# A transformer block with 16 top-1 experts: a memory region per expert, routing and row scatters inside the attention pipeline, unsplit expert weights, return by gathers

## The chip, the cores and the metric

The kernel runs on one NeuronCore of a Trainium2 chip. Its engines are TensorE (PE, with its weight loads shown as PEld), VectorE (DVE), ScalarE (ACT), GpSimd (POOL) and the queue of SyncE (SP), which issues most of the plain DMAs; ACT and POOL issue DMAs too. They run side by side and meet at semaphores. The metric is the device time of one execution in microseconds; the kernel before takes 283.23 us (median of 3 runs, 281.55 to 284.89).

## The reference

The input `x` is 4 sequences of 1024 tokens with 128 features, so T = 4096 rows. Two layers follow each other, each behind a LayerNorm and each added to its input:

```
q, k = l2norm(heads(n @ Wq + bq)), l2norm(heads(n @ Wk + bk)); v = heads(n @ Wv + bv)
attn = (q k^T) / 1024 ** sigmoid(m)            # 16 heads of 8, no softmax
x    = x + (attn v) @ Wo + bo
h    = layernorm(x)
logits = h @ router_w.T                         # 16 experts, top 1
score  = sigmoid(logit of the chosen expert)
g, u = split((h * score) @ gate_up[e]);  routed = (u * silu(g)) @ down[e]
shared = (silu(h @ shared_gate.T) * (h @ shared_up.T)) @ shared_down.T     # inner width 512
out  = x + shared + routed
```

Attention is linear (no softmax), so q (k^T v) is computed as 128x128 products.

## The kernel before

**Units.** 4096 tokens are 32 tiles of 128 rows and 8 quads of 4 tiles. A stage works on a quad at a time (512 columns). The shared part takes a quad in KC = 4 steps, so 32 steps in all. The routed part sorts rows by expert into slots of 128 rows, each slot of one expert; NG = 12 groups of 4 slots always suffice (48 slots).

**Order of the program.** The order is written out by hand for each engine and stands still; semaphores alone couple the engines.

1. *Attention*, STEPS = 11 steps `s` over the 8 quads, software pipelined: step `s` projects quad `s` (PE `project`, L932), DVE takes q, k, v out of PSUM (`take_qkv`, L682), sums squares per head (L691), floors them with a max (L695) and inverts the roots (L699); POOL scales q and v (`scale_heads`, L378); PE multiplies k by v and, three steps later, attends (`attend`, L970); DVE adds the result to `xres` (L711) and makes the second LayerNorm's scales (L668). POOL also adds the bias `bo` to `xres` (`add_bo`, L387), makes the low half of `hT` (`hT_lo`, L391) and, in steps 2, 4, 6 and 8, of the expert weights (`split_lo`, L397): every fp32 operand of `split_product` (L976 to L978) is held as a high and a low fp32r half, and a product is three passes. ACT makes the high halves (`split_hi`, L519).
2. *Routing*, once for quads 0 to 5 and once for 6 and 7: DVE picks the largest logit (`choose`, L777 to L786), counts rows ahead of each row (L789 to L793) and places them (L797 to L800). POOL and ACT scale the rows of `h_rows` by their score (L405).
3. *Scatters of the rows*: POOL issues 32 indirect DMAs (L432), a tile each, from `h_rows` to `x_slots` in memory. Tile t waits until tile t-2 has landed, so at most two are under way:

```
for t in range(NT):
    ...
    if t >= 2:
        pool.wait_ge(scat[t % 2], 16 * (t // 2))
    g.indirect_dma_start(out=x_slots, ..., in_=h_rows[:, t, :], ...).then_inc(scat[t % 2], 16)
```

   Beside them PE, ACT and DVE run the shared part for C1 = 5 quads (`silu_shared` L534, `act_shared` L726, `lo_shared` L731, `down_shared` L1014 to L1016, `turn_y` L1065, `add_shared` L848).
4. *Experts*, 12 groups: SP loads a group when all scatters have landed (one DMA of 258 KB), PE transposes it (L1108), gate-up product in split form (L976 to L978), ACT silu (L619), DVE product (L889), PE transposes (L1132), DVE copies (L893), PE down product (L1124), ACT copy into `yg` (L623). Each group's result goes back by 4 indirect DMAs on POOL (L441) to the rows of its tokens in `y_rows`, paced as the first scatters are, behind the same ring of two.
5. *The other 3 shared quads*, and when all 48 result scatters have landed, SP loads `y_rows` in 8 straight DMAs, POOL adds quads 0 to 3 (L447) and DVE quads 4 to 7 (`add_experts`, L843), and `out` is stored.

In the rows below, `x_slots` and `y_rows` are tensors in memory, `bank` is one of four PSUM banks, `quad_banks` the other four, `pos` the row of `x_slots` that a token goes to, `home` the row that a result returns to.

## Time and profile before

| what | value |
|---|---|
| median of 3 runs | 283.23 us |
| profiled execution: span from first to last instruction | 289.3 us |
| mean granted TensorE clock | 0.863 of full |
| busy: PE, DVE, POOL, ACT | 205.9, 166.4, 142.6, 123.6 us |
| POOL, issues of y scatters (L441) | 48, 46.6 us |
| POOL, issues of x scatters (L432) | 32, 32.5 us |

The span stands for the time of the profiled execution; nothing outside it is listed. It is 6.1 us above the median of the runs. PE is the busiest engine over the whole, at 71%, but the share is an average over stages that have different limits, which the windows below take apart. The page's chain of waits gives PE 22%, DVE 19%, "issue" (time that the profile gives no reason for) 19%, an unknown releaser 14%, POOL 12%.

### The profile page before, as it was taken

What the parts mean: (1) busy time and instruction counts of PE and PEld (TensorE: products, weight loads), DVE (VectorE), ACT (ScalarE), POOL (GpSimd) and SP (SyncE); (2) the same over time, 40 slices, a digit from 0 to 9 for tenths busy, and PEclk for the clock granted to TensorE, in tenths of its full rate; (3) what the DMA queues carried; (4) which work ended last, traced back from release to release, by engine and by line L of the source; (5) the groups of instructions that cost most, each with busy time, mean ns of one, the idle gap of its engine ahead of it and who ended that gap; (6) DMA issues with size and microseconds to landing.
All of it is one profiled execution on the core that took longest, in us unless ns stands there. A gap on an engine that the chain in (4) does not pass through costs nothing.

```text
span 289.3 us, 3485 instructions
## 1 busy us (share of the span) xinstructions
PE 205.9 (71%) x1067; PEld 164.8 (57%) x1067; DVE 166.4 (58%) x401; ACT 123.6 (43%) x238; POOL 142.6 (49%) x148
## 2 busy tenths in 40 slices
PE   1777868898897694889996005999866733539983
PEld 0435646667687573567774004999865632427761
DVE  2179999989863869966667001775832100124665
ACT  3325458565664778355555001454521101024560
POOL 8004747556564227356666640045567666752610
PEclk9999999978975976899999555999997567669999
DMA  4997020520000000011111114244311110102935
GB/s 127 293 386 250 6 70 1 160 60 1 1 2 0 0 0 0 11 39 46 37 48 37 46 37 110 73 106 144 110 48 45 45 54 37 54 27 88 283 94 145
DMA packets 27905, 22.58 MB, mean 78 GB/s; under 512 B 2400, under 2 KB 24944, under 8 KB 27888
## 3 DMA queue, kind: packets, MB, share of 16 engines
q1 hardware_dynamic: 22640, 15.85, 18.8%
q0 software_dynamic: 2560, 5.26, 5.1%
q10 hardware_dynamic: 2688, 1.25, 1.6%
q8 instruction: 9, 0.15, 0.2%
q14 instruction: 8, 0.07, 0.1%
HBM read 11.83 MB, written 10.53 MB: 77 GB/s over the span
## 4 chain that ended last, share of the span: by engine, by line
PE 22%; DVE 19%; issue 19%; another core or an unknown queue 14%; POOL 12%; ACT 7%; DMA 6%; POOLq 0%; DVEq 0%; SPq 0%; ACTq 0%
POOL x_slots L432 6%; DMA x_slots<-h_rows,pos 5%; PE quad_banks L976 3%; PE quad_banks L977 3%; PE quad_banks L978 3%; POOL qkv L378 3%; DVE st L647 2%; DVE qkv L682 2%; DVE ss L691 2%; PE bank L1124 2%; PE bank L1014 2%; PE bank L1108 1%; PE quad_banks L932 1%; DVE ss L695 1%
## 5 line engine op out<-in xcount | busy, mean ns | idle before, releaser
L441 POOL DMA_INDIRECT y_rows<-yg,home x48 | 46.6, 971 | 45.6 <-ACT yg L623 20.9
L432 POOL DMA_INDIRECT x_slots<-h_rows,pos x32 | 32.5, 1016 | 24.5 <-issue 13.8
L726 DVE TENSOR_TENSOR s_act<-quad_banks,sg_act 128x512 f32<-128x512 f32 x32 | 22.0, 690 | 32.6 <-ACT sg_act L534 30.0
L534 ACT ACTIVATE sg_act<-quad_banks 128x512 f32<-128x512 f32 x32 | 19.1, 599 | 43.2 <-PE quad_banks L978 27.8
L378 POOL TENSOR_TENSOR qkv<-qkv,rn 128x512 f32<-128x512 f32 x16 | 16.9, 1078 | 33.3 <-DVE rn L699 33.3
L1124 PE MATMUL bank<-w_dn,e_actT 128*128 x96 | 16.6, 328 | 19.1 <-DVE e_actT L893 19.1
L932 PE MATMUL quad_banks<-w_c,xT 128*128 128x384 f32 x64 | 27.7, 586 | 0.9 <-ACT w_c L543 0.6
L1124 PEld LDWEIGHTS bank<-w_dn,e_actT 128*128 128x128 f32 x96 | 14.7, 234 | 20.9 <-issue 20.9
L731 DVE TENSOR_TENSOR s_spl<-s_act,s_spl 128x512 fp32r<-128x512 f32 x32 | 21.9, 683 | 5.1 <-ACT s_spl L540 4.8
L1014 PE MATMUL bank<-s_spl,sdT 128*128 128x512 f32 x32 | 15.5, 484 | 9.9 <-DVE s_spl L731 9.9
L1108 PE MATMUL bank<-ident,xg 128*128 128x128 f32 x48 | 7.7, 287 | 19.2 <-DMA xg<-x_slots 19.2
L932 PEld LDWEIGHTS quad_banks<-w_c,xT 128*128 128x128 f32 x64 | 14.2, 234 | 11.5 <-issue 4.8
L540 ACT CAST s_spl<-s_act 128x512 fp32r<-128x512 f32 x32 | 19.6, 613 | 2.2 <-DVE s_act L726 2.1
L682 DVE SCALAR_TENSOR_TENSOR qkv<-quad_banks,rs,b_qkv 128x384 f32<-128x384 f32 x32 | 17.3, 595 | 3.8 <-PE quad_banks L932 3.8
L889 DVE TENSOR_TENSOR e_act<-quad_banks,eg_act 128x512 f32<-128x512 f32 x12 | 8.3, 691 | 18.8 <-issue 15.2
L391 POOL TENSOR_TENSOR hT<-hT_raw,hT 128x512 fp32r<-128x512 f32 x8 | 10.3, 1296 | 16.0 <-ACT hT L491 16.0
L1108 PEld LDWEIGHTS bank<-ident,xg 128*128 128x128 f32 x48 | 5.8, 147 | 19.8 <-DMA xg<-x_slots 19.6
L616 ACT CAST xgT<-bank 128x512 fp32r<-128x512 f32 x12 | 7.1, 588 | 23.1 <-PE bank L1108 21.6
L893 DVE COPY e_actT<-bank 128x512 f32<-128x512 f32 x12 | 8.3, 691 | 14.4 <-remote 13.7
L619 ACT ACTIVATE eg_act<-quad_banks 128x512 f32<-128x512 f32 x12 | 7.2, 599 | 20.4 <-remote 14.3
L623 ACT COPY yg<-bank 128x512 f32<-128x512 f32 x12 | 7.0, 586 | 20.2 <-remote 17.9
L647 DVE BATCH_NORM_STATS2 st<-xres 128x6 f32<-128x128 f32 x64 | 13.8, 279 | 2.8 <-DMA xres<-L_attn_x 2.5
(156 smaller groups left out, 582.5 us busy)
## 6 DMA issues: line engine op xcount, KB each, us to landing
x_slots<-w_raw SPq DMA_DIRECT2D x8, 387.0 KB, 6.0
xg<-x_slots SPq DMA_DIRECT2D x12, 258.0 KB
xres<-L_attn_x SPq DMA_DIRECT2D x8, 256.0 KB, 5.6
w_raw<-L_ffn_gate_up_proj SPq DMA_DIRECT2D x4, 512.0 KB, 3.6
h_rows<-y_rows SPq DMA_DIRECT2D x8, 256.0 KB, 4.9
out<-xres SPq DMA_DIRECT2D x4, 256.0 KB, 4.0
out<-xres ACTq DMA_DIRECT2D x4, 256.0 KB, 2.6
y_rows<-yg,home POOLq DMA_INDIRECT x48
```

Source lines behind the costliest of these rows:

```text
L378: g.tensor_tensor(v, v, r, ALU.mult).then_inc(done, 1)
L432: g.indirect_dma_start(out=x_slots, out_offset=bass.IndirectOffsetOnAxis(ap=pos[:, t:t + 1], axis=0), in_=h_rows[:, t, :], in_offset=None) ...
L441: g.indirect_dma_start(out=y_rows, out_offset=bass.IndirectOffsetOnAxis(ap=home[:, n:n + 1], axis=0), in_=yg[:, n, :], in_offset=None).the ...
L534: a.activation(sg_act[:, k % 2], pair[:, 2 * (k % 2)], ACT.Silu).then_inc(s_silu, 1)
L540: a.copy(s_spl[:, k % 2, 0], s_act[:, k % 2]).then_inc(s_hi, 1)
L647: last = v.bn_stats(st[:, t, :], xres[:, t, :])
L682: last = v.scalar_tensor_tensor(out=qkv[:, c % QRING, j, :], in0=pair[:, j, 0:QKV], scalar=rs1[:, t:t + 1], in1=b_qkv[:], op0=ALU.mult, op ...
L726: v.tensor_tensor(s_act[:, k % 2], pair[:, 2 * (k % 2) + 1], sg_act[:, k % 2], ALU.mult).then_inc(s_act_rdy, 1)
L731: v.tensor_tensor(s_spl[:, k % 2, 1], s_act[:, k % 2], s_spl[:, k % 2, 0].bitcast(F32), ALU.subtract).then_inc(s_spl_rdy, 1)
L932: last = te.matmul(pair[:, j, 0:QKV], xT[:, c % 2, P * j:P * j + P], w_c[:], start=True, stop=True)
L1014: te.matmul(ps_yT[:], w[:, 0], h[:, 0], start=(k == 0), stop=False)
L1124: mm = te.matmul(ps_yg[:, P * j:P * j + P], e_actT[:, (par - 3) % 2, P * j:P * j + P], dn_cols[:, bass.ds(cols[j], D)], start=True, stop=True)
```

## The change

- `x_slots` gets a region of 4224 rows for every expert, so that a row's place depends on its expert and on the rows ahead of it in that expert alone, not on the totals of the other experts. Only the first 128 rows of each region are zeroed (1 DMA of 1 MB instead of 8 of 387 KB).
- Routing is done per quad: DVE's `choose(s - 5)` and `place(s - 5)` stand inside the attention steps, POOL counts and scatters quad `s - 6` there. Rows are scattered unscaled, with their top logit as the 129th value.
- The totals give a table of 48 slots (first row, expert's column); a group's load becomes 4 DMAs of one slot, at addresses read from the table. The score is computed after the load (`score`: three small DVE operations, a silu on ACT, a reciprocal and a product), and POOL multiplies the rows by it (`score_rows`).
- Expert weights stay fp32: no split, one product of 4 x 256 columns per group instead of three passes; ACT's `split_hi` and POOL's `split_lo` are gone.
- `bo` enters as one product of 2 rows ahead of `attend`, and POOL's `add_bo` is gone. The max of L695 becomes a Relu on ACT.
- C1 is 2 instead of 5: six shared quads stand behind the experts.
- A group's result is stored straight into `y_slots` by SP (ring of 4 in `yg`). When all 12 stores have landed, POOL gathers the rows by 32 indirect DMAs into `h_rows`, and DVE adds all 8 quads.

```diff
-    C1 = 5
+    C1 = 2
+    YRING = 4
+    REG = T + P
-    x_slots = nc.dram_tensor("x_slots", (SLOTS, W), F32, kind="Internal").ap()
+    x_slots = nc.dram_tensor("x_slots", (E * REG, W), F32, kind="Internal").ap()
 # SP
+            def load(g):
+                first = slot_values(0, g, mybir.EngineType.SP, E * REG - P)
+                if g == 0:
+                    sp.wait_ge(zero_st, 16)
+                    for landed in scat:
+                        sp.wait_ge(landed, 16 * NT // 2)
+                for j in range(Q):
+                    sp.dma_start(xg[:, g * Q + j, :], x_slots[bass.ds(first[j], P), :]).then_inc(xg_ld[g], 16)
+            def store(g):
+                sp.wait_ge(yg_rdy, g + 1)
+                sp.dma_start(y_slots[g * Q * P:(g + 1) * Q * P, :]..., yg[:, g % YRING]).then_inc(y_st[g % YRING], 16)
+            sp.wait_ge(table_rdy, 1)
+            for g in range(NG):
+                if g != 1:
+                    load(g)
+            for g in range(NG):
+                store(g)
 # POOL
             for s in range(STEPS):
...
                 for c in turned(s):
                     hT_lo(c)
-                if live(s - 1):
-                    add_bo(s - 1)
-                if s in SPLIT_STEPS:
-                    split_lo(SPLIT_STEPS.index(s))
+                if live(s - 5):
+                    count(s - 5)
+                if live(s - 6):
+                    scatter(s - 6)
+            scatter(STEPS - 6)
+            for c in range(STEPS - 5, NQ):
+                count(c)
+                scatter(c)
+            for g_no in range(NG):
+                score_rows(g_no)
+            for stored in y_st:
+                pool.wait_ge(stored, 16 * NG // YRING)
+            pool.wait_ge(y_row_rdy, 1)
             for t in range(NT):
...
                 if t >= 2:
+                    pool.wait_ge(back[t % 2], 16 * (t // 2))
+                g.indirect_dma_start(out=h_rows[:, t, 0:D], out_offset=None, in_=y_slots,
+                                     in_offset=bass.IndirectOffsetOnAxis(ap=y_row[:, t:t + 1], axis=0)
+                                     ).then_inc(back[t % 2], 16)
 # ACT
+            yT_copy(C1 - 1)
+            load_second()
+            score(0)
+            score(1)
+            turned_rows(0)
+            for g in range(NG + 2):
+                if g < NG:
+                    gate(g)
+                if g + 2 < NG:
+                    score(g + 2)
+                if g + 1 < NG:
+                    turned_rows(g + 1)
+                if g >= 2:
+                    take_y(g - 2)
 # DVE
-                dve.wait_ge(ss_done, c + 1)
-                v.tensor_scalar(ss[:, c % 2], ss[:, c % 2], 1e-24, None, ALU.max).then_inc(ssum, 1)
+            def choose(c):
+                dve.wait_ge(log_mm, c + 1)
...
+                link(v.tensor_reduce(top, logits, AX.X, ALU.max))
+                link(v.tensor_tensor(far[:], logits, top.unsqueeze(2).broadcast_to([P, Q, E]), ALU.is_lt))
...
+            def score(g):
+                dve.wait_ge(xg_ld[g], 16 * Q)
+                here = slice(g * Q, g * Q + Q)
+                link(v.tensor_tensor(logit_inv[:, here], xg[:, here, D], xg[:, here, D], ALU.mult))
+                link(v.tensor_scalar(logit_inv[:, here], logit_inv[:, here], TINY, APART, ALU.is_lt, ALU.mult))
+                v.tensor_tensor(logit[:, here], logit_inv[:, here], xg[:, here, D], ALU.add).then_inc(logit_rdy, 1)
+                dve.wait_ge(logit_rdy, g + 1)
+                link(v.reciprocal(logit_inv[:, here], logit[:, here]))
+                dve.wait_ge(logit_act, g + 1)
+                v.tensor_tensor(esc[:, here], logit_silu[:, here], logit_inv[:, here], ALU.mult).then_inc(esc_rdy, 1)
 # PE
+            def gate_up_experts(g):
+                cols = slot_values(1, g, mybir.EngineType.PE, (E - 1) * D)
+                pe.wait_ge(gT_sb, g + 1)
...
+                for j in range(Q):
+                    mm = te.matmul(gate_up_banks(g % 2)[:, j, :], xgT[:, g % 2, P * j:P * j + P],
+                                   gu_cols[:, bass.ds(cols[j] * 2, F2)], start=True, stop=True)
+            for g in range(NG + 2):
+                if g < NG:
+                    gate_up_experts(g)
+                if g + 1 < NG:
+                    rows_of(g + 1)
+                if g >= 2:
+                    down_experts(g - 2)
+                if 1 <= g <= NG:
+                    turn_act(g - 1)
```

**POOL, from the last attention steps to the end.** Each row is an instruction of POOL's queue with its line, tiles and count. Before:

```order
L378 TENSOR_TENSOR qkv<-qkv,rn 128x4x128 x2
L391 TENSOR_TENSOR hT<-hT_raw,hT 128x512
L387 TENSOR_TENSOR xres<-xres,b_o 128x512
L397 TENSOR_TENSOR w_gu<-w_raw,w_gu 128x1024
L391 TENSOR_TENSOR hT<-hT_raw,hT 128x512 x3
L405 TENSOR_TENSOR h_rows<-h_rows,score 128x4x128 x5
L432 DMA x_slots<-h_rows,pos 6144x129 x32
L441 DMA y_rows<-yg,home 10241x128 x48
L447 TENSOR_TENSOR xres<-xres,h_rows 128x512 x4
```

Now, from step 8 of the attention on (steps 6 and 7 begin as this one does, each with 4 scatters):

```order
L342 TENSOR_TENSOR qkv<-qkv,rn 128x4x128 x2
L346 TENSOR_TENSOR hT<-hT_raw,hT 128x512
L354 TENSOR_TENSOR seen<-seen,incl 128x16
L362 DMA x_slots<-h_rows,pos 67584x129 x4
L346 TENSOR_TENSOR hT<-hT_raw,hT 128x512
L354 TENSOR_TENSOR seen<-seen,incl 128x16
L362 DMA x_slots<-h_rows,pos 67584x129 x4
L346 TENSOR_TENSOR hT<-hT_raw,hT 128x512 x2
L354 TENSOR_TENSOR seen<-seen,incl 128x16
L362 DMA x_slots<-h_rows,pos 67584x129 x8
L384 TENSOR_TENSOR xg<-xg,esc 128x4x128 x12
L396 DMA h_rows<-y_slots,y_row 128x128 x32
```

The 32 scatters have moved from behind the attention into its steps 6 to 10 and the stretch behind them, the 48 result scatters are gone, and 32 gathers stand at the end of the queue.

**ACT, a group of the experts, with the semaphores that each row waits for.** Before, two groups of the steady loop:

```order
L616 CAST xgT<-bank 128x512 [waits gT_mm]
L619 ACTIVATE eg_act<-quad_banks 128x512 [waits e_gu_mm]
L623 COPY yg<-bank 128x512 [waits e_dn_mm]
L616 CAST xgT<-bank 128x512 [waits gT_mm]
L619 ACTIVATE eg_act<-quad_banks 128x512 [waits e_gu_mm]
L623 COPY yg<-bank 128x512 [waits e_dn_mm]
```

Now, two groups:

```order
L550 ACTIVATE eg_act<-quad_banks 128x512 [waits e_act_rdy,e_gu_mm]
L538 ACTIVATE logit_silu<-logit 128x4 [waits logit_rdy]
L544 COPY xgT<-bank 128x512 [waits e_gu_mm,gT_mm]
L556 COPY yg<-bank 128x512 [waits y_st0,e_dn_mm]
L550 ACTIVATE eg_act<-quad_banks 128x512 [waits e_act_rdy,e_gu_mm]
L538 ACTIVATE logit_silu<-logit 128x4 [waits logit_rdy]
L544 COPY xgT<-bank 128x512 [waits e_gu_mm,gT_mm]
L556 COPY yg<-bank 128x512 [waits y_st1,e_dn_mm]
```

The copy of a group's transposed rows (L544) has moved from ahead of a silu to behind it, and a small silu of the score, which waits for DVE, stands between the two.

## Rows read from the trace of the kernel before

**Rows 1.** The page's first line

```profile
span 289.3 us, 3485 instructions
```

**Rows 2.** Windows: from:to us, length; PE, PEld, DVE, ACT, POOL busy; clock, DMA share, GB/s

```profile
30.00:82.00 52.00, 44.27 (x255) 34.12 (x255) 47.54 (x139) 31.25 (x68) 31.74 (x26) 0.92 0.13 41
...
119.60:175.90 56.30, 34.95 (x155) 26.86 (x155) 26.84 (x43) 20.25 (x37) 32.51 (x32) 0.85 0.15 47
175.90:210.00 34.10, 32.55 (x256) 30.86 (x257) 21.45 (x50) 16.18 (x28) 11.44 (x12) 0.95 0.38 101
210.00:257.00 47.00, 23.62 (x111) 20.50 (x109) 7.93 (x14) 7.02 (x13) 30.80 (x33) 0.72 0.12 47
```

**Rows 3.** Groups of DVE's instructions, 30 to 82 us: busy, mean ns, idle before

```profile
L695 DVE TENSOR_SCALAR ss<-ss 128x128 f32<-128x128 f32 x6 | 4.5, 748 | 0.2
```

**Rows 4.** Timelines of POOL and DVE in the attention: start, duration, what

```profile
69.81 2.36 POOL L397 TENSOR_TENSOR w_gu<-w_raw,w_gu 128x1024 fp32r<-128x1024 f32 x1
...
70.13 2.06 DVE L668 SCALAR_TENSOR_TENSOR nm<-mv,rs 128x4 f32<-128x4 f32 x1
```

**Rows 5.** Timeline of POOL, attention steps 6 to 10; idle before and releaser in brackets

```profile
67.35 1.27 POOL L391 TENSOR_TENSOR hT<-hT_raw,hT 128x512 fp32r<-128x512 f32 x1 [2.72 <-ACT hT L491]
...
73.13 2.11 POOL L378 TENSOR_TENSOR qkv<-qkv,rn 128x512 f32<-128x512 f32 x2 [0.96 <-DVE rn L699]
...
100.04 2.67 POOL L391 TENSOR_TENSOR hT<-hT_raw,hT 128x512 fp32r<-128x512 f32 x2 [5.55 <-ACT hT L491]
```

**Rows 6.** Timeline of POOL, the first scatter of rows

```profile
119.63 1.53 POOL L432 DMA_INDIRECT x_slots<-h_rows,pos  x1 [5.13 <-DVE pos L800]
```

**Rows 7.** Chain of waits, end of the scatters and first load: start, duration, what

```profile
170.55 2.27 DMA x_slots<-h_rows,pos
...
172.89 2.96 DMA xg<-x_slots
...
181.33 0.20 PE quad_banks L976
```

**Rows 8.** Timeline of PE: a quad's projection; down products of two successive groups

```profile
41.73 2.85 PE L932 MATMUL quad_banks<-w_c,xT 128*128 128x384 f32 x8
...
190.47 1.05 PE L1124 MATMUL bank<-w_dn,e_actT 128*128 x8
...
193.68 1.06 PE L1124 MATMUL bank<-w_dn,e_actT 128*128 x8
```

**Rows 9.** Timeline of DVE: a small operation on 4 columns

```profile
193.36 0.16 DVE L883 TENSOR_TENSOR home<-xg,away 128x4 int32<-128x4 f32 x1
```

**Rows 10.** Timelines of PE, DVE and ACT in the second half of the experts

```profile
226.74 1.06 PE L1132 MATMUL bank<-ident,e_act 128*128 128x128 f32 x4
...
235.50 0.69 DVE L893 COPY e_actT<-bank 128x512 f32<-128x512 f32 x1 [4.43 <-remote]
...
239.75 0.60 ACT L534 ACTIVATE sg_act<-quad_banks 128x512 f32<-128x512 f32 x1 [5.11 <-remote]
...
251.10 0.60 ACT L534 ACTIVATE sg_act<-quad_banks 128x512 f32<-128x512 f32 x1 [5.11 <-remote]
```

**Rows 11.** Timelines of POOL and ACT: two result scatters, 31 apart, and the last result copy

```profile
210.86 0.96 POOL L441 DMA_INDIRECT y_rows<-yg,home  x1 [0.78 <-DMA y_rows<-yg,home]
...
253.75 0.96 POOL L441 DMA_INDIRECT y_rows<-yg,home  x1 [0.30 <-issue]
...
256.06 0.59 ACT L623 COPY yg<-bank 128x512 f32<-128x512 f32 x1 [4.36 <-remote]
```

**Rows 12.** Timeline of PE: `turn_y` of shared quads 0 and 3

```profile
126.31 0.60 PE L1065 MATMUL bank<-ident,yT 128*128 128x128 f32 x4
...
153.30 0.60 PE L1065 MATMUL bank<-ident,yT 128*128 128x128 f32 x4
```

**Rows 13.** Chain of waits, the end

```profile
283.68 0.60 ACT yT L590
...
285.81 0.69 DVE xres L843
```

More of the change, by code:

```diff
@@ L626, in _ @@
-            shared(0, C1)
-            over_groups(experts, act, lambda k: silu_shared(C1, k))
-            shared(C1, NQ)
-            for c in range(POOL_FINAL, NQ):
-                act.wait_ge(fin, c - POOL_FINAL + 1)
+            for n in range(C1 * KC + 1):
+                if n < C1 * KC:
+                    silu_shared(n)
+                if n >= 1:
+                    hi_shared(n - 1)
+                if n >= KC and n % KC == 0 and n < C1 * KC:
+                    yT_copy(n // KC - 1)
@@ new lines, in _ @@
+            add_shared(C1 - 1)
+            score(0)
+            score(1)
+            y_rows()
+            for g in range(NG + 1):
+                if g < NG:
+                    gated(g)
+                if g + 2 < NG:
+                    score(g + 2)
+                if g >= 1:
+                    turned_act(g - 1)
+            for n in range(C1 * KC, NQ * KC + 1):
+                shared_step(n, C1, NQ)
+                if n > C1 * KC and n % KC == 3:
+                    add_experts(n // KC - C1)
@@ L901, in _ @@
+            for c in range(NQ - C1, NQ):
+                if c == NQ - 1:
+                    add_shared(NQ - 1)
+                add_experts(c)
         @block.tensor
@@ L1089, in columns @@
-            def columns(g, which):
-                _, vals = nc.values_load_multi_w_load_instructions(
-                    eid_flat[0:1, bass.ds((g * 2 + which) * Q, Q)], engines=(mybir.EngineType.PE,), min_val=0,
-                    max_val=(E - 1) * D,
-                    skip_runtime_bounds_check_because="VectorE made them as D * min(a count of experts, E - 1)")
-                return vals
-            eid_flat = eid[:].rearrange("o g s j -> o (g s j)")
-            gu_cols = w_gu[:].rearrange("p s e c -> p s (e c)")
@@ L1135, in _ @@
[L1135 to L1140 removed]
+            count_before(NQ - 2)
+            for n in range(C1 * KC):
+                if n >= 2:
+                    gate_up_shared(n)
+                if n == 2:
+                    count_before(NQ - 1)
+                if n == 3:
+                    count_all()
+                if n == 4:
+                    turn_table()
+                if n >= KC and n % KC == 2:
+                    turn_y(n // KC - 1)
+                if n >= 2:
+                    down_shared(n - 2)
```

821 lines of the change are left out of this document (376 added, 445 removed).

## The prediction, made before the change was run

> **What bounds the kernel now.** I read the page's shares first, then busy time by stage, then the chain of waits at the seams between stages, then single rows.
>
> The span is 289.3 us [rows 1], 6.1 over the median of the runs; I build the sum against the span and take 6.1 off at the end. In the attention DVE is busy 47.54 of 52.00 us, more than any other engine [rows 2]: that stage is DVE's. From 119.6 to 175.9 us no engine is near full: PE 34.95, DVE 26.84, POOL 32.51 of 56.30 [rows 2]. There POOL's 32 scatters set the end. The first is issued at 119.63 [rows 6], the last at 170.55 [rows 7], so one every (170.55 - 119.63) / 31 = 1.64 us; the last lands 2.27 us later and the first load of an expert group takes 2.96 [rows 7]. The experts are at first PE's: 32.55 busy of 34.10 us [rows 2], a group every 193.68 - 190.47 = 3.21 us [rows 8]. From 210 to 257 us PE has only 23.62 busy of 47.00, DVE 7.93, ACT 7.02, POOL 30.80 [rows 2]. There the signals of finished PE work come late: transposes end at 226.74 + 1.06 = 227.80, and the DVE copy that needs nothing else starts at 235.50, 7.7 us later, its wait unexplained ("remote") [rows 10]; two successive silus of the shared part stand 11.35 us apart [rows 10]. It goes with result scatters at 1.38 us each, 210.86 to 253.75 for 31 of them [rows 11]. The end: from the last copy of ACT at 283.68 to 289.3 are 5.6 us, and from the end of the last addition, 285.81 + 0.69, to 289.3 are 2.8 us for the output store [rows 13, 1].
>
> **The change, part by part.**
>
> *Scatters inside the attention.* POOL issues the first behind `hT_lo(2)`, which ends at 67.35 + 1.27 = 68.6 [rows 5]; with the count and the hand-off I take 69.5. From there POOL's queue is one chain: 31 paces of 1.64 = 50.8 us, and between the scatters two times (2.11 for scaling heads, 1.27 for `hT_lo`, 0.2 for the count) = 7.2, then 1.27 + 0.2, then 2.67 + 0.2, then 0.4 = 12.0 us in all [rows 5, 9]. Last issue at 69.5 + 50.8 + 12.0 = 132.3, landed at 134.6 (before: 172.8). The routing of the last quad doesn't hold it up: `hT_lo(7)` ends after 4 scatter blocks at about 107 instead of 102.7, and its scatter is not due before 127. The pauses are POOL's, so q and v scaling (before at 73.13 [rows 5]) come some 3 us later in two steps; the attention's tail runs later by that, but no longer sets the end.
>
> *DVE in the attention.* Gone: the max of L695, 0.75 us per quad [rows 3], and waits beside `split_lo`: a 4-column operation that takes 0.16 us elsewhere [rows 9] took 2.06 beside the 2.36 us POOL operation [rows 4]. Added: 10 small operations per quad. Their lower bound is 0.16 each [rows 9], the upper bound 0.69 (512 columns [rows 10]); on 64 columns I take 0.25 to 0.3, the lower end being nearer: 2.8 us a quad, of which only quads 0 to 2 fall in steps where DVE also projects. Lost 3 x 2.8 = 8.4, won 8 x 0.75 and two such waits of 1.9, 9.8: about nothing. ACT loses the high halves, POOL the low ones and `add_bo`; all are under DVE's cover, and nothing is gained by them beyond this. The extra 2-row product for `bo` is 0.4 us per quad on a PE with 8 us free in 52 [rows 2], the Relu (at most 0.6 [rows 10]) lies on an ACT with 20 us free [rows 2].
>
> *First load and start of the experts.* 134.6 + 2.96 = 137.6. Before the first product stands the score: five DVE operations of 0.2, a small silu of 0.3 (between 0.16 and 0.60 [rows 9, 10]), POOL's product of 512 columns 1.06 (half of 2.11 [rows 5]), transposes 0.9, a copy 0.6 and hand-offs of 0.3: 4.2 us. First gate-up at 141.8, against 181.33 [rows 7]: 39.5 us earlier. The shared part before it is 2 quads of 9.0 us ((153.30 - 126.31) / 3 [rows 12]) and ends well before.
>
> *A group of the experts.* The new order on ACT makes a ring: gate-up(g) on PE, its silu, DVE's product, then DVE's `score(g+2)`, ACT's small silu which stands ahead of the copy of the next rows, the copy, gate-up(g+1). Gate-up is four fp32 products of 256 columns. A quad's projection, four of 384 recorded as 8 passes, takes 2.85 [rows 8], in proportion 1.9; the down product, four of 128 recorded as 8 passes, takes 1.05 [rows 8], doubled 2.1. The bounds are 1.7 (the projection less some fixed cost) and 2.1; I take 1.8, near the projection, whose columns are the nearer. Then: result out 0.3, silu 0.60, product 0.69 [rows 10], three small DVE operations 0.6 [rows 9], small silu 0.3, copy 0.60 [rows 10], hand-offs 0.2: 5.1 us, so I carry 5.0 per group against 3.21 before. Eleven periods: 55.0, last gate-up at 196.8. Behind it 1.8 + 0.3 + 0.6 + 0.7 + transposes 1.06 + copy 0.7 + down 1.06 + copy 0.6 [rows 8, 10] = 6.8: results out at 203.6. SP's stores queue behind 44 small loads; each needs at least the issue but all are issued long before, since loads wait for the scatters alone. Store 3.0 (by the 258 KB load's 2.96 [rows 7]): 206.6.
>
> *The return.* No gather is in the trace. Nearest rows: 1.38 a piece for the dense result scatters [rows 11], 1.64 for the row scatters [rows 7]; the ring of two is the same. I take 1.64: the row scatters share their time with shared steps, as the gathers will. 31 x 1.64 = 50.8, landing 2.3, addition 0.7, output 2.8: 206.6 + 56.6 = 263.2.
>
> This case's rows give 2.27 us from a scatter's issue to its landing. The Trainium skill ("DMA: Bandwidth & Descriptors", section "Anatomy of one DMA — SWDGE (gpsimd) path") gives about 2.0 us plus bytes / 436 GB/s per DMA of this kind; as an estimate that is 2.15 us for 64 KB, and with two under way the return would be near the one above.
>
> *The last six shared quads.* They start when PE has done its last down product, 203.0: 6 x 9.0 = 54.0 [rows 12], 2.5 to fill the pipe and 5.6 for the tail [rows 13]: 265.1. Two chains end together; the later one sets it.
>
> **Sum.** 265.1 - 6.1 = **259**, that is 24 us or 9% faster. About 38 us come from the scatters that move forward, 20 from the missing late signals; 20 go to the longer group period and 15 to the three quads moved behind.
>
> Own range of this case: 1.38 instead of 1.64 ends the scatters 8 us sooner; gate-up at 2.1, hand-offs and small operations at 0.1 more each add 0.9 a group, 10 us; at 0.16 a small operation 2 us go, and the gathers at 1.38 can't help PE's chain: 249 to 270.
>
> **Rivals.**
>
> *(a) The experts stay PE's.* If DVE's and ACT's small operations slip into gaps, the group costs PE's 3.2 plus 0.3 for the wider product, 3.5. For: PE was 95% busy in rows 2. Against: the silu of the score stands between two operations in the same queue. 11 x 1.5 = 17 us less, 242.
>
> *(b) The late signals stay in the expert loop.* Before, 12 groups took 256.65 - 181.33 = 75 us [rows 7, 11]; my stretch is 203.6 - 141.8 = 62. If they come from the loop and not from POOL's DMAs, 13 us more: 272. Against: none in the first 30 us of the stage [rows 2].
>
> *(c) DVE and POOL block each other in the attention.* Twelve scatters are issued while DVE is 91% busy. If each issue waits for one full-width DVE operation, 0.69 [rows 10], the chain ends 12 x 0.69 = 8 us later: 267. For it speaks the 2.06 beside the 2.36 [rows 4]. The Trainium skill ("SBUF — State Buffer", section "SBUF: two separate sides") calls the port pair that VectorE and GpSimd share an exclusive lock, and says that descriptors of DMAs from GpSimd's queue can't be written while VectorE holds it. By that rule this rival would be the likely one; the issue's even 0.96 us [rows 11] was read in stages where DVE is half idle, and so doesn't test it.
>
> *(d) The other side: the gathers bring the late signals.* Mechanism: dense indirect DMAs on POOL, in runs at 1.38 or less, are what delays PE's signals [rows 10, 11]; in the row scatters at 1.64 none was late. Before, only the experts' second half lay beside them; now six shared quads would. A shared step then takes 11.35 us for one or two [rows 10] instead of 2.25. Gathers from 206.6 to 252 let 4 to 8 steps through, 15 to 19 of 24 are left: 252 + 34 to 43 + 5.6 = 291 to 300, minus 6.1: 285 to 294, I take 290. It decides where a gather lands so fast that POOL never waits for the ring, issuing with gaps of 0.30 us [rows 11]. For: the coincidence from 210 us on. Against: at 1.64 nothing of it, and a gather reads where a scatter writes.
>
> **How the numbers follow.** Forecast 0.54, (a) 0.11, (b) 0.12, (c) 0.09, (d) 0.12, 0.02 for anything else. Within 1% (about what a measurement of this kernel can tell from no change) is 280 to 286: the lower edge of (d) and (b) with (c), 0.07. Slower: the rest of (d) and the unknown, 0.14. Faster: 0.79. The range takes in the forecast's own, (b), (c) and most of (a), and reaches up to the foot of (d): 243 to 284.
>
> **What would show it.** Scatters inside the attention: first POOL scatter near 69.5 us, the last near 132, the first gate-up near 142; if DVE's window shows waits and the scatters are 2 us apart or more, it is (c). Group period: successive gate silus on ACT 5.0 apart, 3.5 in (a). Late signals: "remote" waits of 4 us on ACT and DVE, in the expert loop (b) or beside the gathers (d), and there shared silus far over 2.25 us apart. The gathers: 32 of them, 1.64 apart, starting near 207. The forecast is wrong if the attention itself grows by more than 5 us, if the loads of single slots are paced by SP's queue, or if gathers take over 2 us each.

## The result: slower, 301.56 us against 283.74 us

The changed kernel takes 301.56 us (median of 4 runs, 297.92 to 303.46) where the kernel before, on the same chip, takes 283.74 us (281.55 to 284.89). The ratio is 1.0585, 95% interval [1.0479, 1.0691]. The forecast was 259 us. Two of its four runs, 302.58 and 303.46 us, lie over 1.5% above its fastest, and without them its median is 299.24 us, 2.3 us lower. The profiled execution of the changed kernel has a span of 298.8 us and took 300.55 us: here the time of an execution is its span plus 1.75 us. In the runs of the kernel before that have both numbers the difference is 1.8 to 2.4 us, so a span of 289.3 [rows 1] belongs to an execution of 291 to 292 us, slower than any run of the kernel before that was timed beside it.

The first line of the page, and the windows of the changed kernel, cut at its own seams: attention up to 82 us, its rest, the last scatters, the start of the experts, the experts, the end. Columns are those of rows 2.

```profile
span 298.8 us, 3655 instructions
```

```profile
30.00:82.00 52.00, 42.52 (x214) 31.57 (x215) 39.97 (x135) 26.61 (x60) 18.52 (x20) 0.82 0.11 33
82.00:127.20 45.20, 36.77 (x153) 30.89 (x152) 24.75 (x91) 17.81 (x38) 22.47 (x25) 0.61 0.06 20
127.20:152.20 25.00, 17.76 (x69) 13.71 (x68) 12.56 (x44) 5.13 (x9) 16.31 (x19) 0.71 0.13 43
152.20:169.30 17.10, 10.28 (x45) 7.11 (x43) 7.95 (x21) 5.78 (x12) 1.28 (x2) 0.90 0.52 116
169.30:231.00 61.70, 48.81 (x288) 41.92 (x289) 25.04 (x77) 20.64 (x45) 11.57 (x11) 0.95 0.25 67
231.00:298.80 67.80, 56.61 (x238) 41.45 (x236) 39.58 (x62) 29.16 (x55) 32.36 (x32) 0.95 0.25 66
```

Against rows 2 the attention has lost its bound: DVE was busy 47.54 of 52.00 us, now 39.97, and in the 45 us behind it 24.75. PE is the busiest there, 36.77 of 45.20 us, but at a granted clock of 0.61, where a row can take nearly twice as long (5.47 against 2.85 us below). No engine is full. The stage is now held by waits between engines, and by what the lower clock behind them costs PE.

**The attention ring.** Rows of DVE and PE around the seam of two steps, put together in order of time; the brackets hold the idle time ahead and what ended it.

```profile
64.65 5.47 PE L903 MATMUL quad_banks<-w_c,xT 128*128 128x384 f32 x8
...
77.95 0.16 DVE L696 TENSOR_TENSOR pos<-rank,near 128x4 int32<-128x4 f32 x1
78.26 0.35 PE L950 MATMUL bank<-rwT,hT 128*128 128x16 f32 x1 [1.81 <-DVE pos L696]
...
81.37 4.01 PE L903 MATMUL quad_banks<-w_c,xT 128*128 128x384 f32 x8
84.24 2.32 DVE L633 SCALAR_TENSOR_TENSOR qkv<-quad_banks,rs,b_qkv 128x384 f32<-128x384 f32 x4 [5.27 <-PE quad_banks L903]
```

The reader is to see who waits for whom. DVE places quad 1 at 77.95, the last thing but one of its step. Only then may PE start the router product of quad 2 (L950), since both use one PSUM bank, and only behind its 12 products (three passes for each of four tiles) comes the projection of the next quad. Meanwhile DVE has nothing left and idles 5.27 us. The projection of 2.85 us [rows 8] takes 5.47 and 4.01: PE had waited 1.9 us for DVE's running count and 2.0 us for `pos` ahead of the first, and the granted clock over its 5.45 us is 0.50. Successive projections start 16.7 us apart.

**The count behind the scatters.** Rows of POOL and PE:

```profile
137.93 0.96 POOL L362 DMA_INDIRECT x_slots<-h_rows,pos  x1 [0.35 <-DMA x_slots<-h_rows,pos]
138.90 0.24 POOL L354 TENSOR_TENSOR seen<-seen,incl 128x16 f32<-128x16 f32 x1
```

```profile
134.43 0.54 PE L975 MATMUL bank<-incl,before 128*128 128x16 f32 x2
139.19 0.61 PE L977 MATMUL bank<-seen,ones 128*128 128x16 f32 x2 [4.23 <-POOL seen L354]
...
144.93 0.61 PE L982 MATMUL bank<-seen,ones 128*128 128x16 f32 x2 [1.10 <-POOL seen L354]
```

PE stands 4.23 us for an addition of 0.24 us, because POOL issues eight scatters first. Shared products are queued behind on PE.

**The scatters and the start of the experts.** POOL's first scatter, the last low half of `hT`, and the last scatter:

```profile
76.26 1.18 POOL L362 DMA_INDIRECT x_slots<-h_rows,pos  x1 [0.18 <-issue]
...
125.86 1.30 POOL L346 TENSOR_TENSOR hT<-hT_raw,hT 128x512 fp32r<-128x512 f32 x1 [0.56 <-ACT hT L442]
...
149.86 0.96 POOL L362 DMA_INDIRECT x_slots<-h_rows,pos  x1 [0.52 <-DMA x_slots<-h_rows,pos]
```

```profile
162.76 0.59 ACT L487 COPY yT<-bank 128x512 f32<-128x512 f32 x1 [1.79 <-PE bank L1019]
163.55 2.13 ACTq L533 DMA_DIRECT2D xg<-x_slots  x4
```

```profile
167.47 1.09 PE L1090 MATMUL bank<-ident,xg 128*128 128x128 f32 x4 [3.41 <-POOL xg L384]
169.32 3.62 PE L1099 MATMUL quad_banks<-w_gu,xgT 128*128 x8 [0.77 <-ACT xgT L544]
```

The last rows land near 152, but the first expert product starts at 169.32: the second shared quad ends only at 162.8, and the loads in ACT's queue and the scores in ACT's and DVE's queues stand behind it.

**The group period.** ACT, one group to the next:

```profile
207.11 0.60 ACT L550 ACTIVATE eg_act<-quad_banks 128x512 f32<-128x512 f32 x1 [1.68 <-PE quad_banks L1099]
208.94 0.21 ACT L538 ACTIVATE logit_silu<-logit 128x4 f32<-128x4 f32 x1 [1.23 <-DVE logit L844]
209.06 0.57 ACT L544 COPY xgT<-bank 128x512 f32<-128x512 f32 x1
...
211.79 0.60 ACT L550 ACTIVATE eg_act<-quad_banks 128x512 f32<-128x512 f32 x1 [1.68 <-PE quad_banks L1099]
```

One group takes 4.68 us, with 1.23 of them ahead of the small silu. The page has no wait named "remote" any more.

**The return and the last shared quads.** First and last gather, and ACT's copies of two successive shared quads:

```profile
234.10 1.01 POOL L396 DMA_INDIRECT h_rows<-y_slots,y_row  x1 [14.21 <-DMA y_slots<-yg]
...
282.06 1.19 POOL L396 DMA_INDIRECT h_rows<-y_slots,y_row  x1 [0.30 <-issue]
```

```profile
273.56 0.58 ACT L487 COPY yT<-bank 128x512 f32<-128x512 f32 x1 [1.87 <-PE bank L1019]
...
283.49 0.58 ACT L487 COPY yT<-bank 128x512 f32<-128x512 f32 x1 [1.87 <-PE bank L1019]
```

31 gathers in 47.96 us are 1.55 each. A shared quad takes 9.93 us instead of 9.0 [rows 12], and ACT waits 1.87 us ahead of each copy.

### The profile page after: what moved, and what is told of

The parts are those of the page before. It is cut to its first block, busy times and chain, and to the rows that moved or that the text cites. A ratio compares the mean times of both kernels' runs of the same rounds, so it can differ in the third digit from the quotient of the medians.

```text
span 298.8 us, 3655 instructions
## 1 busy us (share of the span) xinstructions
PE 229.3 (77%) x1059; PEld 176.4 (59%) x1059; DVE 168.6 (56%) x487; ACT 116.4 (39%) x238; POOL 109.3 (37%) x134
## 3 DMA queue, kind: packets, MB, share of 16 engines
q1 hardware_dynamic: 25476, 14.46, 20.1%
## 4 chain that ended last, share of the span: by engine, by line
PE 46%; DVE 25%; ACT 8%; DMA 8%; issue 8%; POOL 4%; SPq 1%; ACTq 1%; POOLq 0%; DVEq 0%
PE quad_banks L1099 9%; PE quad_banks L903 7%; PE bank L1017 3%; PE bank L944 3%; PE quad_banks L950 3%; PE quad_banks L951 3%; PE quad_banks L952 3%; DMA x_slots<-h_rows,pos 3%; DVE st L598 3%; DVE ss L642 2%; DVE e_act L830 2%; DVE s_spl L741 2%; DVE s_act L736 2%; DMA xres<-L_attn_x 2%; PE bank L1019 2%
## 5 line engine op out<-in xcount | busy, mean ns | idle before, releaser
L396 POOL DMA_INDIRECT h_rows<-y_slots,y_row x32 | 32.4, 1011 | 31.0 <-DMA y_slots<-yg 14.2
L736 DVE TENSOR_TENSOR s_act<-quad_banks,sg_act 128x512 f32<-128x512 f32 x32 | 22.1, 689 | 27.6 <-ACT sg_act L477 26.9
L362 POOL DMA_INDIRECT x_slots<-h_rows,pos x32 | 31.3, 980 | 13.3 <-DMA x_slots<-h_rows,pos 7.8
L1099 PE MATMUL quad_banks<-w_gu,xgT 128*128 x96 | 26.8, 428 | 11.9 <-ACT xgT L544 11.9
L384 POOL TENSOR_TENSOR xg<-xg,esc 128x512 f32<-128x512 f32 x12 | 12.8, 1071 | 56.2 <-DVE esc L848 56.2
L903 PE MATMUL quad_banks<-w_c,xT 128*128 128x384 f32 x64 | 29.6, 619 | 0.9 <-ACT w_c L490 0.6
L1099 PEld LDWEIGHTS quad_banks<-w_gu,xgT 128*128 128x128 f32 x96 | 19.1, 209 | 17.2 <-issue 14.6
L440 ACT COPY hT_raw<-bank 128x512 f32<-128x512 f32 x8 | 4.7, 585 | 34.7 <-PE bank L893 34.7
L950 PE MATMUL bank<-rwT,hT 128*128 128x16 f32 x32 | 10.2, 320 | 8.6 <-DVE pos L696 8.0
L1017 PEld LDWEIGHTS bank<-s_spl,sdT 128*128 128x128 f32 x32 | 6.3, 196 | 16.4 <-DVE s_spl L741 16.1
L426 ACT ACTIVATE h_rows<-xres,nm,rs 128x128 f32<-128x128 f32 x32 | 13.1, 480 | 4.0 <-DVE nm L619 4.0
```

What stands on the lines that cost most here:

```text
L362: g.indirect_dma_start(out=x_slots, out_offset=bass.IndirectOffsetOnAxis(ap=pos[:, t:t + 1], axis=0), in_=h_rows[:, t, :], in_offset=None) ...
L396: g.indirect_dma_start(out=h_rows[:, t, 0:D], out_offset=None, in_=y_slots, in_offset=bass.IndirectOffsetOnAxis(ap=y_row[:, t:t + 1], axis ...
L736: v.tensor_tensor(s_act[:, n % 2], pair[:, 2 * (n % 2) + 1], sg_act[:, n % 2], ALU.mult).then_inc(s_act_rdy, 1)
L903: last = te.matmul(pair[:, j, 0:QKV], xT[:, c % 2, P * j:P * j + P], w_c[:], start=True, stop=True)
L950: te.matmul(out, lhs[:, 0], rhs[:, 0], start=True, stop=False)
L1017: te.matmul(ps_yT[:], w[:, 0], h[:, 0], start=(k == 0), stop=False)
```

## The experiments

Kernels of one group ran on one chip beside the kernel before, whose median was 282.05 us for the first four, 282.49 for the next four, 282.21 for the next three and 280.63 for the last. The changed kernel's 301.56 stands beside 283.74, and its runs are 5.5 us apart, so differences to it of under 3 us say nothing, and each "less than the changed kernel" below would be 2.3 us smaller against 299.24. The fifth to eighth and the last ran on one chip, the others on a second one.

### The router product one step later

```diff
+                if 0 <= s - 5 < NQ - 2:      # behind project(s) and attend
+                    route(s - 5)
-                for c in turned(s):
-                    route(c)                 # quads 6 and 7 stay here
```

> The changed kernel, but PE issues the router product of quad c one step later, behind the next quad's projection and the attend product, so that its wait for place(c-1) on DVE no longer holds the projection. Theory R (a ring PE - DVE - PE through this wait stretches attention steps to 12 to 16 us): steps shrink by 3 to 5 us, hT_lo of the last quad ends near 110 instead of 127 us, the last scatter is issued near 138 instead of 149.9, the time falls by 8 to 15 us. Rival L (DVE and POOL block each other, or POOL's scatters delay its scaling of q and v): attention stays as long as it is, time within 2 us.

Measured 289.84 us (ratio to before 1.0317 [1.0218, 1.0416]), 11.7 less than the changed kernel. Projections in this kernel, row of PE:

```profile
60.62 2.85 PE L903 MATMUL quad_banks<-w_c,xT 128*128 128x384 f32 x8
...
71.19 4.39 PE L903 MATMUL quad_banks<-w_c,xT 128*128 128x384 f32 x8
```

```profile
141.44 0.96 POOL L362 DMA_INDIRECT x_slots<-h_rows,pos  x1 [0.32 <-DMA x_slots<-h_rows,pos]
```

The step at that place shrinks from 16.7 to 10.6 us; the last low half of `hT` ends at 118.1 instead of 127.2, the last scatter is issued 8.4 us sooner. The ring is real; how much of the gain is the wait itself and how much the higher clock once it is gone, the run doesn't divide. The attention is not as short as was expected (110): see the scatters below.

### The count on DVE

```diff
 # POOL
-                if live(s - 5):
-                    count(s - 5)
...
 # DVE, at the end of choose(c)
...
+                v.tensor_tensor(seen[:, c + 1], seen[:, c], incl[:, c % 2, :, Q - 1], ALU.add).then_inc(seen_rdy, 1)
```

> The changed kernel, but the running count of rows per expert (one 128x16 addition per quad) is done by DVE right behind the scan instead of by POOL. Theory Q (PE's queue waits twice for a count that stands behind 4 or 8 scatters in POOL's queue, with shared products queued behind: gaps of PE near 135 to 139 and 140 to 145 us): shared steps before the experts come some 6 to 8 us sooner, first gate-up 3 to 8 us sooner, time falls by 3 to 8 us. Rival L: the scatters alone set the start of the experts, time within 2 us.

Measured 294.31 us (1.049 [1.0383, 1.0596]), 7.3 less. PE's product that stood 4.23 us now has no wait ahead of it, and the first expert silu comes at 168.61 instead of 172.98:

```profile
136.33 0.59 PE L976 MATMUL bank<-seen,ones 128*128 128x16 f32 x2
```

### The score behind the copy of the rows

```diff
                 gate(g)
-                if g + 2 < NG:
-                    score(g + 2)
                 if g + 1 < NG:
                     turned_rows(g + 1)
+                if g + 2 < NG:
+                    score(g + 2)
```

> The changed kernel, but in the expert loop ACT copies the next group's transposed rows before the small silu of the score, not behind it. Theory S (the period of 4.68 us is the ring through that silu and the three DVE operations ahead of it): period falls to 3.5 to 3.8 us, the time by 8 to 13 us. Rival P (the period is PE's own work: 8 passes of the fp32 gate-up, transposes, down): period stays over 4.4 and the time within 3 us.

Measured 292.98 us (1.0433 [1.0319, 1.0547]), 8.6 less. Successive silus of ACT:

```profile
194.12 0.60 ACT L550 ACTIVATE eg_act<-quad_banks 128x512 f32<-128x512 f32 x1 [1.36 <-PE quad_banks L1099]
...
197.94 0.60 ACT L550 ACTIVATE eg_act<-quad_banks 128x512 f32<-128x512 f32 x1 [1.30 <-PE quad_banks L1099]
```

The twelve silus are 3.4 to 4.0 us apart, 3.8 in the mean, instead of 4.68. So the period was the ring through the score, as theory S has it. What is left is PE's: from 190 to 214 us it is busy 23.37 of 24.00 us at full clock, where it was busy 18.91 in the changed kernel. PE's own period is thus about 3.8, the upper edge of what was expected.

### All three

> All three edits together. If R, Q and S hold and add up: attention shorter by 12 to 17 us, shared steps in front no longer held, period 3.5 to 3.8: 20 to 34 us less than the changed kernel, so 268 to 281 us. If the gathers behind the experts then set the end with the shared quads, no less than 265. Rival L and P: over 295.

Measured 269.81 us (0.9619 [0.9526, 0.9712]): 31.8 less than the changed kernel, where the three alone sum to 27.6. They add up. Whether they give more than their sum isn't shown: the median of the changed kernel, uncertain by some us, stands once in the one number and three times in the other.

### The copy of yT one shared step later

```diff
-                if n >= KC and n % KC == 0 and n < C1 * KC:
+                if n >= KC and n % KC == 1 and n < C1 * KC:
                     yT_copy(n // KC - 1)
...
-                if n >= (C1 + 1) * KC and n % KC == 0:
+                if n >= (C1 + 1) * KC and n % KC == 1 and n < NQ * KC:
                     yT_copy(n // KC - 1)
+            yT_copy(NQ - 1)
```

> The three edits together (269.8 us), and ACT's copy of yT stands one shared step later, as the kernel before has it. In the profile of the three edits a shared quad behind the experts takes 9.93 us (silus 243.60 to 253.53) against 9.0 before, and ACT idles 1.9 us ahead of each such copy. Theory Y (the order of ACT's queue costs it): a quad goes to 9.0, six quads give 5 to 6 us, time 263 to 265. Rival G (the gathers beside it cost it: contention, or their chain sets the end): a quad stays over 9.7, time within 2 us.

Measured 264.97 us against 282.49 before, 4.8 less than the three edits alone (on another chip, where the kernel before differs by 0.4). Rows of ACT:

```profile
234.44 0.59 ACT L484 COPY yT<-bank 128x512 f32<-128x512 f32 x1
...
243.43 0.59 ACT L484 COPY yT<-bank 128x512 f32<-128x512 f32 x1
```

A quad takes 8.99 us with gathers beside it at the same pace: the order of ACT's queue was the cost, not the gathers.

### Three shared quads in front

The only edit is C1 = 3.

> As the one with the later yT copy, and C1 = 3: three shared quads stand ahead of the experts instead of two. In the profile of the three edits PE waits 7 us between the last shared step in front and the first transposes, for landing, load and score. If PE's chain sets the end, the quad fills that gap: 3 to 7 us less than the later yT copy alone (257 to 261). If the start of the gathers sets the end (it moves back by 2 to 3 us), no change or up to 2 us slower.

Measured 270.07 us, 5.1 slower than with C1 = 2. The expectation missed, on the side of its second case and beyond it. Gathers of this kernel, the first and the last:

```profile
211.96 1.01 POOL L393 DMA_INDIRECT h_rows<-y_slots,y_row  x1 [13.73 <-DMA y_slots<-yg]
...
262.21 0.94 POOL L393 DMA_INDIRECT h_rows<-y_slots,y_row  x1 [2.46 <-DMA h_rows<-y_slots,y_row]
```

With C1 = 2 they run from 206.55 to 254.43. I had the start 2 to 3 us later, it is 5.4; a gap at the start of the experts that comes from order (load and score queued behind the shared steps) moves with the quads and isn't filled by another. The gathers' end then sets the end: the span of 268.7 us ends 6.5 us behind the last issue, against 11.8 us with C1 = 2.

### The scatters behind the attention

```diff
-                if live(s - 6):
-                    scatter(s - 6)
-            scatter(STEPS - 6)
-            for c in range(STEPS - 5, NQ):
+            for c in range(NQ):
                 scatter(c)
```

> The three edits together (269.8 us), but all 32 row scatters stand behind the attention in POOL's queue, as before the change; routing stays inside. This undoes one part alone. Expected: attention ends 8 to 12 us sooner (last hT_lo near 104 instead of 114), since POOL's scaling of q and v no longer waits behind 4 scatters; the scatters run from 105 to 157, the first expert product comes some 15 us later than 150; the time rises by 10 to 16 us. If scatters inside the attention gave nothing, the time stays within 3 us.

Measured 292.47 us, 22.7 more than with the scatters inside (269.81). Rows of POOL:

```profile
112.74 1.30 POOL L346 TENSOR_TENSOR hT<-hT_raw,hT 128x512 fp32r<-128x512 f32 x1 [0.56 <-ACT hT L436]
114.23 1.18 POOL L362 DMA_INDIRECT x_slots<-h_rows,pos  x1 [0.19 <-DVE pos L692]
...
160.27 0.96 POOL L362 DMA_INDIRECT x_slots<-h_rows,pos  x1 [0.37 <-DMA x_slots<-h_rows,pos]
```

Moving the scatters into the attention is worth 22.7 us, where I had expected 10 to 16. They cost the attention 1.0 us (its last low half ends at 115.06 with them, 114.04 without), where I had expected 8 to 12: wrong. The 1.0 is not clear of noise: in profiles of later kernels with the same attention that end lies between 111.8 and 115.9. Neither POOL's order nor a block between POOL and DVE stretches the attention by much. This can be seen in the rows as well. In the kernel with the three edits, whose scatters stand inside, a block of four is issued while DVE is 94% busy (4.03 of 4.30 us; columns of rows 2):

```profile
69.40:73.70 4.30, 3.42 (x11) 2.21 (x12) 4.03 (x13) 2.60 (x8) 3.24 (x4) 0.68 0.09 31
```

```profile
69.44 1.18 POOL L362 DMA_INDIRECT x_slots<-h_rows,pos  x1 [0.18 <-issue]
70.92 0.97 POOL L362 DMA_INDIRECT x_slots<-h_rows,pos  x1 [0.30 <-issue]
72.30 0.96 POOL L362 DMA_INDIRECT x_slots<-h_rows,pos  x1 [0.41 <-DMA x_slots<-h_rows,pos]
```

The first issue of a block takes 1.18 us behind the attention too (114.23 above), and the others keep their 0.96 [rows 11].

What keeps the attention at 114 us against 102.7 [rows 5] was not tested, but the rows point at PE and its clock: from 82 to 104 us PE is busy 19.68 of 22.00 us at a granted clock of 0.53 in this kernel, 19.54 at 0.64 with the scatters inside, and 17.56 at 0.80 in the kernel before. POOL is busy only 4.68 us of it here.

### The kernel before with plain stores for its results

```diff
-                for n in range(Q * g_no, Q * g_no + Q):
-                    g.indirect_dma_start(out=y_rows, out_offset=..., in_=yg[:, n, :], in_offset=None)
...
+                g.dma_start(y_rows[lo:lo + Q * P, :]..., yg[:, Q * g_no:Q * g_no + Q, :])
```

> The kernel before, but a group's result goes to memory by one plain DMA from POOL's queue instead of 4 indirect ones: the return of rows to their tokens is left out, all else stands. Theory D (dense indirect DMAs on POOL make the signals of finished PE work late from 210 us on): no remote waits of 4 us, the expert stage ends 13 to 20 us sooner (near 237 to 243 instead of 256.7), time 262 to 270. Rival (another cause in that loop): silus stay 5 to 11 us apart there, and only the end of the scatters goes: time within 4 us of before.

This kernel leaves out the return of rows to their tokens, so it bounds a cost and is no version to use. Measured 255.79 us against 282.49: 26.7 less, more than the 12 to 20 expected. The seven runs of the kernel before beside it reach from 276.76 to 286.62 us, and against the shortest of them the gain is 21.0 us. Silus of ACT, and the window that answers to the last of rows 2:

```profile
198.33 0.60 ACT L619 ACTIVATE eg_act<-quad_banks 128x512 f32<-128x512 f32 x1 [0.86 <-PE quad_banks L978]
201.52 0.60 ACT L619 ACTIVATE eg_act<-quad_banks 128x512 f32<-128x512 f32 x1 [0.84 <-PE quad_banks L978]
```

```profile
210.00:224.00 14.00, 13.48 (x92) 11.99 (x92) 7.78 (x14) 6.73 (x12) 3.75 (x5) 1.00 0.24 95
```

No remote wait is left, the group stays at 3.2 us, and the last result copy ends at 220.95 instead of 256.65 [rows 11]. The late signals belong to the indirect result scatters: with them gone the lateness is gone. The edit changes three things at once, 12 issues instead of 48, rows that lie side by side, and no index per row; which of them does it was not separated. In the kernel before the first late signal comes at 201.88 us, 12 us behind the first result scatter at 189.71, so "none in the first 30 us of the stage" in the prediction holds for 26 us only.

### Four gathers under way

```diff
-        back = [sem("back0"), sem("back1")]
+        back = [sem(f"back{i}") for i in range(4)]
-                if t >= 2:
-                    pool.wait_ge(back[t % 2], 16 * (t // 2))
+                if t >= 4:
+                    pool.wait_ge(back[t % 4], 16 * (t // 4))
```

> As the one with the later yT copy (265.0 us), but four gathers may be under way instead of two. POOL then issues them at up to 1.26 us each instead of 1.55 (0.96 and the 0.30 gap), 31 x 1.26 = 39 us instead of 48. Theory N (dense indirect DMAs of any kind on POOL make finished PE work be signalled late, the other-side rival of the prediction): remote waits of 4 us and more beside the gathers, shared silus 5 us or more apart, time 275 to 295. Rival M (it needs scatters, which write; gathers don't do it): no such waits; PE's six shared quads set the end already, time 263 to 266.

Measured 265.50 us (0.9478 [0.9372, 0.9585]), the same as with two.

```profile
206.00 1.01 POOL L393 DMA_INDIRECT h_rows<-y_slots,y_row  x1 [13.72 <-DMA y_slots<-yg]
207.31 0.96 POOL L393 DMA_INDIRECT h_rows<-y_slots,y_row  x1 [0.30 <-issue]
...
245.48 1.17 POOL L393 DMA_INDIRECT h_rows<-y_slots,y_row  x1 [0.30 <-issue]
```

1.27 us a gather, each behind the one before it with nothing between them but 0.30 us of issue, denser than the result scatters of before, and not one remote wait: theory N fell, rival M holds. PE's six shared quads set the end: the span of 265.6 us goes on for 20.1 us behind the last gather's issue.

### C1 = 3 with all loads on SP, and with four gathers

> As the one with C1 = 3 (270.1 us), but group 1 is loaded by SP too, not by ACT behind its shared steps. With C1 = 3 the last gather is issued at 262.2 us, 8 us later than with C1 = 2, since the first expert product waits for load and score behind a third quad. If the load in ACT's queue is what holds the start: first product 2 to 3 us sooner, time 267 to 268. If DVE's score behind its shared steps holds it: time within 1 us.

Measured 268.63 us, 1.4 less than with the load on ACT, but its four runs (265.35, 266.19, 271.06, 274.14) are 8.8 us apart, and against the two shorter ones it would be 4.3. The first expert silu is at 159.23 instead of 161.20, but the attention of this profile also ended 4.1 us sooner (111.84 against 115.92), which the edit doesn't touch. So what the place of the load is worth stays open.

> C1 = 3, loads on SP, and four gathers under way. If the chain of gathers set the end with C1 = 3, 9 us shorter gathers give 5 to 9 us: 260 to 264, with PE's five shared quads next. If dense gathers bring late signals (theory N): 270 to 290.

Measured 263.80 us (0.9405 [0.9285, 0.9525]): the lowest median, 6% under the kernel before. It can't be told from C1 = 2 with two or four gathers (264.97 and 265.50). It is 4.8 under the same with two gathers under way, but only 2.0 under the two shorter runs of that kernel, 265.35 and 266.19. That with C1 = 3 it is the gathers' chain that sets the end is seen more surely in the profiles: with two under way the span ends 6.5 us behind the last gather's issue (257.80 to 264.3), room for its landing, the addition and the store; with four it ends 11.7 us behind (251.11 to 262.8), and PE sets the end, as it did with C1 = 2.

### The first scores ahead of the last shared products

On top of that, `score(0)`, `score(1)` and the first transposes stand one shared step sooner on DVE, ACT and PE.

> C1 = 3, loads on SP, four gathers (263.8 us), and the scores of groups 0 and 1 are computed one shared step before the end of the third quad on DVE and ACT, the first transposes go ahead of the last down product on PE. In the profile without this 9.7 us lie between the last yT copy of the third quad and the first gate silu (151.2 to 160.9), filled by load, score, POOL's product and transposes one after the other. If this serial start is what is left: first gate silu 4 to 5 us sooner (near 156), results and gathers too, time 258 to 260. If the load from memory or the clock after the gap holds it: within 2 us.

Measured 265.04 us (0.9428 [0.9314, 0.9541]), no gain. PE's first gate-up product, without and with the edit:

```profile
157.30 3.52 PE L1099 MATMUL quad_banks<-w_gu,xgT 128*128 x8 [0.76 <-ACT xgT L540]
```

```profile
157.49 3.71 PE L1102 MATMUL quad_banks<-w_gu,xgT 128*128 x8
```

It starts at the same time and takes 3.5 to 3.7 us against 1.99 in the next group, at a granted clock of 0.55 and 0.53, near the lower level, in both. The copy of the rows was ready at 153.3, but DVE's scores had pushed its own last product, and with it PE's last shared product, to 154.25. Expected was 156 for the silu, it came at 161.23: the wait was moved, not filled.

## Why the prediction was wrong, step by step

Predicted span 265.1 us, measured 298.8: 33.7 us. The other 8.9 of the 42.6 us between forecast and median are the 6.1 that I took off, the 1.75 between span and time, and 1.0 between the profiled execution and the median. Of the terms below, 17.6 and 9.9 stand ahead of the first expert product, 0.1 comes back in the groups and 6.3 stands behind them. Taking the distance of one profile to its median for a constant was wrong: the profile of before was of an execution longer than any of the runs.

1. *Scatters inside the attention: wrong, 17.6 us.* "From there POOL's queue is one chain": it was not. The last scatter was predicted landed at 134.6 and landed near 152.2; POOL waited for PE and DVE ahead of each block. The first scatter was 6.8 us late (76.26 against 69.5). Inside the blocks of four the pace was 1.36 us where 1.64 was forecast, 32.6 us for 24 paces instead of 39.4; the seven passages from block to block took 41.0 us instead of 23.5. So the term of 12.0 us for what stands between the scatters is the one that failed, and a pace that was set too high hid part of it. The forecast costed DVE's ten added operations (most 0.15 to 0.29 each, a few 0.5 to 0.7, one beside POOL 1.15; the 2.8 us a quad were right) but never listed the waits that `route` got: on `pos_rdy` of the quad before, in front of the next projection. It is the failed step. Moving the router product with this wait behind the projection gave 11.7 us (9.4 against the changed kernel's 299.24), of the 17.6. The clause about DVE, "lost 8.4, won 9.8: about nothing", argued from busy time while the stage had changed from a full engine to a ring.
2. *The count: its wait not in the prediction, 7.3 us.* The sum had 0.2 us for each count on POOL. But a wait was added on PE for an operation at the back of POOL's queue; the text named what POOL's chain holds up only for q and v (3 us), and the scatters as a whole cost the attention near 1.0.
3. *Start of the experts: wrong, 9.9 us more.* I had the shared part in front "well before" the load. It ended at 162.8, held by points 1 and 2, and load and score stand behind it in the queues.
4. *Group period: right in its mechanism, a little high.* 5.0 predicted, 4.68 measured in the steady part. From the first product to the last result it is 61.7 us where 61.8 was forecast, and that closeness is luck: to the first silu 3.7 us instead of 2.1, eleven periods 51.7 instead of 55.0, behind the last silu 6.4 instead of 4.7. The ring through the score is shown by the third experiment. Rival (a) is out in this kernel, since the small silu did stand in the way; PE's own period, 3.8 rather than its 3.5, appears when the copy is put ahead of the score.
5. *Gathers: right.* 1.55 us each against 1.64, and landing as scatters do. They start at 234.10 where the stores' end at about 234 lets them; the length was 48 us, forecast 50.8. The prediction also says that 2.15 us from issue to landing with two under way comes near the same; it doesn't, it would be 1.08 us each and 33 us.
6. *Shared quads and the end: forecast 6.3 us too short,* 5.6 of them 6 x 0.93. 9.0 was taken from the order of before; the changed order puts the yT copy ahead of a silu that was ready, 9.93. The fifth experiment gives back 8.99.
7. *Late signals gone: right, mostly.* The rival (b) is out: none in the loop. Rival (d), the other side, named the wrong mechanism: gathers at 1.27 us do nothing to PE's signals. Its chance of 0.12 was, with 0.02 for anything else, the only one on the side that came true, and the time came from another reason. Rival (c) is out too: scatters cost the attention 1.0 us, not 8, and beside a DVE that was 94% busy an issue kept its 0.96 to 1.18 us. The Trainium skill ("SBUF — State Buffer", section "SBUF: two separate sides") gives the lock a condition that the prediction left out: it is DVE's operations in a 2-port mode, or with two SBUF inputs beside a GpSimd operation that reads SBUF, that take the shared ports. So the runs show that it had no price for the scatters here; they don't speak against it as a rule. Between ordinary operations of the two the trace agrees with it: `pos`, 0.16 us elsewhere, ends at 127.18 just as POOL's `hT_lo` of 125.86 does (127.16).

```profile
126.03 1.15 DVE L696 TENSOR_TENSOR pos<-rank,near 128x4 int32<-128x4 f32 x1
```

With the three edits and the copy put right the kernel takes 264.97 us, and its profile has a span of 266.2 us beside the forecast's 265.1. That is no proof of the forecast. The first gate silu comes at 153.67 where 143.9 was forecast, 9.8 us late, and from there to the last result it takes 49.8 us where 59.7 was forecast, because the third edit removes a ring that the forecast had counted; so the gathers start at 206.55 where 206.6 was forecast. Two misses cancel. Of the 36.6 us between the changed kernel and this one, some 24 belong to waits that the forecast did not list (11.7, 7.3 and 4.8), 8.6 to the ring through the score, which it had, and the rest isn't assigned.

## What to carry to other kernels

When work is moved into a pipeline, list for every engine each new wait and what stands behind it in that queue, and walk one step round the engines: a wait for the previous item of another engine, in front of the next item's first product, turns two busy engines into a ring, whatever each one's busy time says. Put a product that nobody waits for in this step behind the one that the other engine needs next, keep small operations that others wait for out of a queue of slow DMA issues, and put a copy that frees the next product ahead of side work that waits. A reordering of a few lines was worth 29 to 32 us here, more than the whole change had lost.

## What the runs showed of the hardware that I had not expected

- Indirect result scatters from POOL at 1.38 us each go with signals of PE's finished work 4 to 8 us late (3.7 to 7.7 from the end of the transposes to DVE's copy, in the kernel before from 212 us on); plain stores don't, and indirect gathers at 1.27 us don't. Why the result scatters do it stays open, and so does why the row scatters don't, which ran at 1.49 to 1.64 us, inside the blocks of four of the changed kernel even at 1.36.
- After waits of PE of 3 to 4 us in sum the first gate-up product takes 3.52 to 3.71 us against 1.99: nearly twice, as it would at 1.2 instead of 2.4 GHz. The granted clock over it is 0.55 (from 157.3 to 160.8 us, C1 = 3 with four gathers) and 1.00 over the next one. So the stretch behind a wait pays once more. What this is worth over the whole kernel was not measured.
- An indirect DMA from POOL keeps the queue 0.94 to 1.2 us, mostly 0.95, and then 0.30 us of issue, for gathers and scatters alike; with four under way that is the whole pace.
